# The predicated copies of a sorting network on VectorE walk their longest dimension innermost

## The chip, the cores and the metric

The kernel runs on one core of a Trainium2 chip. The metric is the device time of one execution in microseconds (us), the median of several runs; of the kernel before three runs are known.

## The reference, cut to what matters

The program is a two-layer relational graph convolution over 625 nodes of 768 features, followed by a feed-forward part with sixteen experts. The graph part and the output layers are not touched here. What matters is the gate of each expert:

```
for i in range(16):
    gate_feature = hidden_states * pe[i] @ gate_w + gate_b
    gate_weight, gate_idx = top_k(gate_feature, 384)      # of 768, for each of 625 tokens
    gate_weight = softmax(gate_weight)
    gathered = take_along_axis(hidden_states, gate_idx)
    y = y + (silu(x @ eg_w[i]) * (x @ eu_w[i])) @ ed_w[i]  # x = gathered * gate_weight
```

So for each expert and each token the largest 384 of 768 gate features are wanted in order, and with each of them the hidden value of the same column.

## The kernel before, in words

**The sort.** The kernel does the top_k as a sorting network on VectorE. The 625 tokens lie as 125 partitions by 5 tokens (`NT = 5`), so that each partition sorts 5 times 768 values at once. The 768 values of a token are three runs of 256 (`BLK = 3`), interleaved: the word at place i of run b of token t lies at `(i*3 + b)*5 + t` in a partition. One place of the three runs and five tokens is 15 words (`GRP = 15`). A stage of the network compares places that are `dist` apart; the function `pair` gives its two sides as views. For a stage of the first part (kind "sort", distances from 128 down to 1) a side has rows of `dist * 15` words at a pitch of twice that, except where `dist` is the length of the run that is merged. After the stage "join" the two best runs of each token lie in `key_top` and `pay_top` without the third run, and a place is 5 words: there the rows are `dist * 5` words at a pitch of twice that. In "join" and "flip" the outputs are contiguous, seen as rows of 5 words.

**Keys and payloads.** Keys (`key`, `key_top`) are the gate features, payloads (`pay`, `pay_top`) the hidden values. A unit of work is a stage or half of one, up to 960 words in a partition, in `UNITS`. For each unit VectorE does four instructions: the larger keys (a maximum, L1616), the smaller keys (a minimum, L1626), and two predicated copies that move the payloads under a mask, the first by `first_pays` (L1637, L1643 or L1649, after the kind of stage), the second by `second_pays` (L1657 or L1666). TensorE makes the mask in PSUM (L1218) from a seed that ScalarE puts there (L1507) and the larger keys, with a product by minus the identity: where the seed was the larger one the mask is zero. ScalarE (L1520) copies a part of the old payloads aside, and GpSimd computes the other part of the second payloads with a sum and a difference of integers (L1319, L1327), so the second copy on VectorE covers only part of the unit (`shares`).

**The order of the work.** The order is written out. There are an opening turn (74 units), fifteen regular turns (93 units each, thirteen of them in a loop) and a closing turn (19 units). A regular turn weaves the first part of one expert's sort with the last part of the sort of the expert before it, so that two chains alternate on VectorE: larger keys of unit u, second copy of unit u-2, smaller keys of u, first copy of unit u-1. TensorE does the experts' matrix products in between the masks. Each engine waits on semaphores of the others (`mask_made`, `seeded`, `moved`, `pays_done` and so on).

**The views.** `part_of` halves a stage, `in_banks` and `seed_of` give the mask the same dimensions as the payloads. A view of a copy has one to three free dimensions, for example `[2, 96, 5]` for the last merge stage: two halves, 96 rows, 5 words. A copy moves its elements in the order of these dimensions, the last one innermost, and that is the order that the change turns.

Of the kernel before, what the change touches and what calls it, by code (L numbers as in the profile page):

```python
# [208 lines left out]
def columns(view):  # L209

    return math.prod(view.shape[1:])


def shaped_like(buffer, view):

    dims = list(view.shape[1:])
    flat = buffer[:, 0:columns(view)]
    if len(dims) == 1:
        return flat
    if len(dims) == 2:  # L220
        return flat.rearrange("p (a b) -> p a b", b=dims[1])
    return flat.rearrange("p (a b c) -> p a b c", b=dims[1], c=dims[2])


def bank_pieces(view):
# [146 lines left out]
def settle(engine, waits_over):  # L372

    engine.sem_inc(waits_over, 1)
# [445 lines left out]
def experts(nc, ffn, chunks, ident, neg_ident, ones, pe_t, h_tok, h_feat, y_tok, gate_w, gate_b, gate_loaded,  # L820
            m1_loaded):
    with ExitStack() as ctx:
# [3 lines left out]
        def sem(name):  # L826
            return ctx.enter_context(nc.semaphore(name))
# [86 lines left out]
        pay_copied, moved, pays_done, pay_set = sem("pay_copied"), sem("moved"), sem("pays_done"), sem("pay_set")  # L914
# [56 lines left out]
        def pay_was(turn, u):  # L971

            home = (u % 2) * (NT * KTOP // 2)
            return shaped_like(pay_side[:, home:NT * KTOP], payloads(turn, u)[0])
# [4 lines left out]
        def seed_of(turn, u):  # L979


            side, bank = compared(turn, u)[0], mask_bank(turn, u)
            dims = list(side.shape[1:])
            if columns(side) <= BANK or len(dims) == 1:
                return shaped_like(bank, side)
            if dims[0] % 2 == 0:
                rows = bank.rearrange("p (n q) -> p n q", n=dims[0])[:, :, 0:math.prod(dims[1:])]
                return rows if len(dims) == 2 else rows.rearrange("p n (m x) -> p n m x", x=dims[2])
            if len(dims) == 3 and dims[0] == 1 and dims[2] // GRP * 16 <= BANK:
                rows = bank.rearrange("p (n m q) -> p n m q", n=1, q=dims[2] // GRP * 16)  # L990
                return rows[:, :, 0:dims[1], 0:dims[2]]
            return shaped_like(bank, side)
# [16 lines left out]
        def mask_of(turn, u):  # L1009
            return seed_of(turn, u).bitcast(I32)  # L1010
# [593 lines left out]
        @block.vector  # L1604
        def _(dve):
            def larger_keys(turn, i, u):
                s, part, _ = turn.units[u]
                dve.wait_ge(seeded, turn.done("units", i, u + 1))
                if s > 0:
                    dve.wait_ge(mask_made, turn.done("units", i, turn.needs[u]))  # L1610
                elif turn is not OPENING:
                    dve.wait_ge(maxed, turn.done("units", i, 0))
                    dve.wait_ge(minned, turn.done("minima", i, 0))
                if s == FLIP or (s == 0 and turn is not OPENING):
                    dve.wait_ge(kept, (i - 1) * NKEPT + 1)
                dve.tensor_tensor(results(turn, u)[0], seed_of(turn, u), compared(turn, u)[1],  # L1616
                                  ALU.max).then_inc(maxed, 1)

            def smaller_keys(turn, i, u):
                smaller, seed, second = results(turn, u)[1], seed_of(turn, u), compared(turn, u)[1]  # L1620
                if smaller is None:
                    return
                if turn.units[u][0] == JOIN:
                    seed, second = [side[:, 0:smaller.shape[1], :] for side in (seed, second)]
                dve.wait_ge(maxed, turn.done("units", i, u + 1))
                dve.tensor_tensor(smaller, seed, second, ALU.min).then_inc(minned, 1)  # L1626

            def first_pays(turn, i, u):

                s, part, parts = turn.units[u]  # L1630
                first, second, larger, _ = payloads(turn, u)
                dve.wait_ge(mask_made, turn.done("units", i, u + 1))
                if s == 0:
                    dve.wait_ge(pay_set, i * NSET + (part + 2))
                    settle(dve, sort_waits)
                    row_b = part_of(pair(h_mixed, None, STAGES[0])[1], part, parts)
                    dve.copy_predicated(first, mask_of(turn, u), row_b)  # L1637
                elif s == FLIP:
                    dve.wait_ge(pays_done, turn.done("units", i, turn.needs[u]))
                    dve.wait_ge(pays_taken, turn.done("sums", i, turn.needs[u]))  # L1640
                    dve.wait_ge(kept, i * NKEPT)
                    settle(dve, sort_waits)
                    dve.copy_predicated(larger, mask_of(turn, u), second).then_inc(pays_done, 1)  # L1643
                else:
                    dve.wait_ge(pay_copied, turn.done("moves", i, u + 1))
                    if turn.shared[u]:
                        dve.wait_ge(pays_added, turn.done("sums", i, u + 1))
                    settle(dve, sort_waits)
                    dve.copy_predicated(larger, mask_of(turn, u), second).then_inc(moved, 1)  # L1649

            def second_pays(turn, i, u):
                s, part, parts = turn.units[u]
                first, second, _, smaller = payloads(turn, u)
                mask = mask_of(turn, u)
                if s == 0:
                    row_a = part_of(pair(h_mixed, None, STAGES[0])[0], part, parts)
                    dve.copy_predicated(second, mask, row_a).then_inc(pays_done, 1)  # L1657
                elif s != FLIP:
                    was = pay_was(turn, u)
                    if s == JOIN:  # L1660
                        mask, was = mask[:, 0:smaller.shape[1], :], first[:, 0:smaller.shape[1], :]
                    elif turn.shared[u]:
                        smaller, mask, was = [shares(side, turn, u)[0] for side in (smaller, mask, was)]
                    dve.wait_ge(moved, turn.done("moves", i, u + 1))
                    settle(dve, sort_waits)
                    dve.copy_predicated(smaller, mask, was).then_inc(pays_done, 1)  # L1666

            def top_key(turn, i, u):
                dve.wait_ge(maxed, turn.done("units", i, u))
                dve.tensor_scalar(neg_max[:, :], key_top[:, 0:NT], -1.0, None, ALU.mult).then_inc(max_ready, 1)  # L1670

            def invert(e):
                dve.wait_ge(exp_ready, e * NT + NT)
                dve.reciprocal(exp_sum[:, :], exp_sum[:, :]).then_inc(inv_ready, 1)

            def sort(turn, i, following=None):

                for u in range(1, turn.streams):
                    if turn is REGULAR and u == INVERT:
                        invert(i - 1)  # L1680
                    larger_keys(turn, i, u)
                    if u > 1:
                        second_pays(turn, i, u - 2)
                    smaller_keys(turn, i, u)
                    if turn is REGULAR and u == SORTED + 1:
                        top_key(turn, i, SORTED + 1)
                    first_pays(turn, i, u - 1)
                if turn.streams:
                    second_pays(turn, i, turn.streams - 2)
                for u in range(max(turn.streams, 1), turn.n):  # L1690
                    larger_keys(turn, i, u)
                    smaller_keys(turn, i, u)
                    first_pays(turn, i, u - 1)
                    second_pays(turn, i, u - 1)
                if following is not None:
                    larger_keys(following, i + 1, 0)
                    smaller_keys(following, i + 1, 0)
                first_pays(turn, i, turn.n - 1)
                second_pays(turn, i, turn.n - 1)

            larger_keys(OPENING, 0, 0)
            smaller_keys(OPENING, 0, 0)
            sort(OPENING, 0, REGULAR)
            sort(REGULAR, 1, REGULAR)
            with dve.Fori(2, NEXP - 1) as i:
                sort(REGULAR, i, REGULAR)
            sort(REGULAR, NEXP - 1, CLOSING)
            sort(CLOSING, NEXP)
            top_key(CLOSING, NEXP, CLOSING.n)
            invert(NEXP - 1)  # L1710
# [120 lines left out]
```

## Time and profile before

| what | value |
|---|---|
| median of 3 runs | 6728.27 us |
| lowest and highest run | 6721.94 and 6728.85 us |
| span of the profiled execution | 6726.6 us |
| VectorE busy over the span | 5167.5 us (77%), 6633 instructions |
| TensorE busy over the span | 5752.0 us (86%) |
| GpSimd busy over the span | 4158.4 us (62%) |
| ScalarE busy over the span | 2659.1 us (40%) |

Of the profiled execution the page gives the span only, and no time of its own beside it; the span is 1.7 us under the median of the runs and lies between the lowest and the highest of them. "Busy" leaves out waiting, and a busy TensorE is not one at its peak. The share of busy time over the span hides that the kernel has different parts: the graph layers up to about 1215 us, then the sort. The rows further down are of the part in which the sort runs.

### The profile page before, as it was taken

To read this page: it belongs to the slowest core of one execution; us is meant where nothing else is said; L and a number is where in the kernel's file an instruction comes from. 1 tells how busy PE (TensorE), PEld (TensorE's weight loads), DVE (VectorE), ACT (ScalarE), POOL (GpSimd) and SP (SyncE) were. 2 spreads that over 40 slices of the span, in tenths; PEclk is the share of its full clock that TensorE was granted. 3 is DMA by queue.
4 is the path that set the end of the run, shared out by engine and by line. 5 is a ranking of instruction groups with operands and counts; after the bars stand their busy time and mean duration, and the time that the engine had idled before them with its cause. 6 is when DMAs were issued, how large, how long until landed. Compare 5 with 4: busy or idle time off the path is not lost. (4 is left out here: it accounts for less than half of the span.)

```text
span 6726.6 us, 73995 instructions
## 1 busy us (share of the span) xinstructions
PE 5752.0 (86%) x16753; PEld 3063.2 (46%) x16753; DVE 5167.5 (77%) x6633; ACT 2659.1 (40%) x4419; POOL 4158.4 (62%) x3692
## 2 busy tenths in 40 slices
PE   7979989788888888888888888888888888889988
PEld 5545545344444444444444444444444444445554
DVE  3012002399999999999999999999999999998840
ACT  0000000244545554454545454545454545554431
POOL 2325005266877777676777777777777777777740
PEclk9989999899999999999999999999999999999989
DMA  3357238100000000000000000000000000001001
GB/s 90 107 132 188 101 99 196 56 15 8 20 23 15 15 15 15 15 15 15 15 15 14 15 14 15 15 19 10 29 0 29 14 15 15 15 29 36 18 32 51
DMA packets 118084, 261.01 MB, mean 39 GB/s; under 512 B 39164, under 2 KB 49922, under 8 KB 117682
## 3 DMA queue, kind: packets, MB, share of 16 engines
q1 hardware_dynamic: 70322, 180.18, 7.6%
q0 software_dynamic: 47360, 77.17, 5.2%
q14 instruction: 357, 2.92, 0.1%
q8 instruction: 45, 0.74, 0.0%
HBM read 222.43 MB, written 34.58 MB: 38 GB/s over the span
## 5 line engine op out<-in xcount | busy, mean ns | idle before, releaser
L1218 PE MATMUL mask_ps<-key,neg_ident 125*125 125x480 f32 (+7 forms) x4128 | 1886.1, 575 | 567.4 <-DVE key L1626 561.2
L1327 POOL TENSOR_TENSOR pay<-pay_side,pay 125x480 int32<-125x480 int32 (+9 forms) x1120 | 1306.1, 1166 | 648.1 <-DVE pay L1649 641.0
L1507 ACT COPY mask_ps<-key 125x960 f32<-125x960 f32 (+7 forms) x1152 | 954.7, 829 | 1698.7 <-DVE pay L1666 1029.3
L1319 POOL TENSOR_TENSOR pay_side<-pay 125x480 int32<-125x480 int32 (+9 forms) x1120 | 1301.1, 1162 | 340.6 <-DVE pay L1666 160.9
L1218 PEld LDWEIGHTS mask_ps<-key,neg_ident 125*125 125x125 f32 x4128 | 732.8, 192 | 1459.8 <-DVE key L1626 994.5
L1649 DVE COPY_PREDICATED pay<-mask_ps,pay 125x960 f32<-125x960 int32 (+6 forms) x1120 | 1240.7, 1108 | 69.0 <-PE mask_ps L1218 35.5
L1616 DVE TENSOR_TENSOR key<-mask_ps,key 125x960 f32<-125x960 f32 (+6 forms) x1120 | 1092.4, 975 | 57.5 <-PE mask_ps L1218 36.2
L1626 DVE TENSOR_TENSOR key<-mask_ps,key 125x960 f32<-125x960 f32 (+6 forms) x1120 | 1092.8, 976 | 0.0
L1218 PE MATMUL mask_ps<-key_top,neg_ident 125*125 125x480 f32 (+3 forms) x1472 | 604.1, 539 | 178.2 <-DVE key_top L1626 168.0
L1165 PE MATMUL slot_ps<-w_exp,hid 128*125 128x384 f32 x1920 | 680.4, 493 | 8.7 <-issue 8.7
L1153 PE MATMUL slot_ps<-gate_w,xs 128*125 128x384 f32 x1920 | 678.8, 490 | 0.0
L1137 PE MATMUL slot_ps<-u_feat,w_exp 128*128 128x312 f32 (+1 forms) x2304 | 668.2, 427 | 0.4 <-ACT u_feat L1397 0.4
L758 POOL DMA_INDIRECT rows_a<-messages_dram,idx_now_a x200 | 242.3, 1212 | 660.6 <-DVE idx_now_a L795 612.7
L657 PE MATMUL ps_msg<-w_rel,h_feat 128*125 128x384 f32 x1920 | 619.7, 486 | 2.4 <-ACT h_feat L589 2.4
L1666 DVE COPY_PREDICATED pay<-mask_ps,pay_side 125x480 f32<-125x480 int32 (+8 forms) x1120 | 592.1, 529 | 4.8 <-DVE pay L1649 2.9
L1520 ACT COPY pay_side<-pay 125x480 f32<-125x480 f32 (+8 forms) x1120 | 508.6, 454 | 147.0 <-POOL pay L1327 97.6
L1137 PEld LDWEIGHTS slot_ps<-u_feat,w_exp 128*128 128x128 f32 x2304 | 439.7, 191 | 245.0 <-issue 119.0
L668 DVE COPY y_out<-ps_msg 125x768 f32<-125x768 f32 x40 | 38.3, 958 | 612.2 <-PE ps_msg L657 612.2
L1165 PEld LDWEIGHTS slot_ps<-w_exp,hid 128*125 128x125 f32 x1920 | 366.4, 191 | 306.9 <-issue 114.7
L1327 POOL TENSOR_TENSOR pay_top<-pay_side,pay_top 125x480 int32<-125x480 int32 (+3 forms) x272 | 327.5, 1204 | 281.1 <-DVE pay_top L1649 276.8
L1153 PEld LDWEIGHTS slot_ps<-gate_w,xs 128*125 128x125 f32 x1920 | 359.1, 189 | 306.1 <-issue 120.8
L1218 PEld LDWEIGHTS mask_ps<-key_top,neg_ident 125*125 125x125 f32 x1472 | 270.8, 199 | 489.1 <-DVE key_top L1626 289.7
(190 smaller groups left out, 5876.3 us busy)
## 6 DMA issues: line engine op xcount, KB each, us to landing
w_rel<-L_gnn_W SPq DMA_DIRECT2D x16, 2304.0 KB, 23.2
w_exp<-L_ffn_ed_w SPq DMA_DIRECT2D x16, 2304.0 KB, 8.4
messages_dram<-y_out SPq DMA_DIRECT2D x16, 1875.0 KB
w_exp<-L_ffn_eg_w SPq DMA_DIRECT2D x16, 1152.0 KB, 5.4
w_exp<-L_ffn_eu_w SPq DMA_DIRECT2D x16, 1152.0 KB, 7.8
root_w<-L_gnn_root SPq DMA_DIRECT2D x2, 2304.0 KB
w_exp<-L_ffn_sg_w SPq DMA_DIRECT2D x4, 1152.0 KB, 6.0
w_exp<-L_ffn_su_w SPq DMA_DIRECT2D x4, 1152.0 KB, 8.8
```

The lines of the kernel that those rows point to most:

```text
L657: last = pe.matmul(slots[n % 2][0:TP, half, 0:HALF], h_feat[:, k, t * TP:(t + 1) * TP], w_rel[j][:, k, cols], start=(k == 0), stop=(k == K ...
L1137: last = pe.matmul(slots[bank][:, 0:count], weight(bank, k), ins[:, k, first:first + count], start=(k == 0), stop=(k == nk - 1))
L1153: last = pe.matmul(slot, xs[:, t % 2, k, :], gate_w[:, k, cols], start=False, stop=(k == KD - 1), skip_group_check=is_set(e, t))
L1165: last = pe.matmul(slots[bank][0:TP, 0:HALF], hid[:, f, t * TP:(t + 1) * TP], down_w[:, f, half * HALF:(half + 1) * HALF], start=(f == 0), ...
L1218: last = pe.matmul(mask, neg_ident[0:TP, 0:TP], operand, start=False, stop=True, skip_group_check=True)
L1319: pool.tensor_tensor(shares(pay_was(turn, u), turn, u)[1].bitcast(I32), first, second, ALU.add).then_inc(pays_added, 1)
L1327: pool.tensor_tensor(second, shares(pay_was(turn, u), turn, u)[1].bitcast(I32), first, ALU.subtract).then_inc(pays_taken, 1)
L1507: act.copy(seed_of(turn, u), compared(turn, u)[0]).then_inc(seeded, 1)
L1616: dve.tensor_tensor(results(turn, u)[0], seed_of(turn, u), compared(turn, u)[1], ALU.max).then_inc(maxed, 1)
L1626: dve.tensor_tensor(smaller, seed, second, ALU.min).then_inc(minned, 1)
L1649: dve.copy_predicated(larger, mask_of(turn, u), second).then_inc(moved, 1)
L1666: dve.copy_predicated(smaller, mask, was).then_inc(pays_done, 1)
```

## The change

A new function turns the views of a predicated copy. It looks for the longest of the output's free dimensions (the first of them, where two are equal) and, where that isn't the innermost already, puts it innermost in output, mask and data alike. All five predicated copies go through it. The same elements are copied under the same mask; only their order within an instruction differs. Copies whose last dimension is the longest, or that have one dimension alone, stay as they are.

```diff
+def longest_last(*views):
+
+    dims = list(views[0].shape[1:])
+    longest = dims.index(max(dims))
+    if longest == len(dims) - 1:
+        return views
+    names = ["abc"[n] for n in range(len(dims))]
+    turned = names[:longest] + names[longest + 1:] + [names[longest]]
+    order = f"p {' '.join(names)} -> p {' '.join(turned)}"
+    return [view.rearrange(order) for view in views]
...
-                    dve.copy_predicated(first, mask_of(turn, u), row_b)
+                    dve.copy_predicated(*longest_last(first, mask_of(turn, u), row_b))
...
-                    dve.copy_predicated(larger, mask_of(turn, u), second).then_inc(pays_done, 1)
+                    dve.copy_predicated(*longest_last(larger, mask_of(turn, u), second)).then_inc(pays_done, 1)
...
-                    dve.copy_predicated(larger, mask_of(turn, u), second).then_inc(moved, 1)
+                    dve.copy_predicated(*longest_last(larger, mask_of(turn, u), second)).then_inc(moved, 1)
...
-                    dve.copy_predicated(second, mask, row_a).then_inc(pays_done, 1)
+                    dve.copy_predicated(*longest_last(second, mask, row_a)).then_inc(pays_done, 1)
...
-                    dve.copy_predicated(smaller, mask, was).then_inc(pays_done, 1)
+                    dve.copy_predicated(*longest_last(smaller, mask, was)).then_inc(pays_done, 1)
```

An example: the first copy of the last merge stage has the view `[2, 96, 5]`, 192 rows of 5 words at a pitch of 10. Turned it is `[2, 5, 96]`: ten walks of 96 elements, each element 10 words behind the last.

## Rows read from the trace of the kernel before

**Rows 1.** The page's engines: busy us, share of the span, instructions.
```profile
PE 5752.0 (86%) x16753; PEld 3063.2 (46%) x16753; DVE 5167.5 (77%) x6633; ACT 2659.1 (40%) x4419; POOL 4158.4 (62%) x3692
```

**Rows 2.** Busy time by stretch, from the first join to the last; columns in its first line.
```profile
core 0: us, PE busy (x) PEld busy (x) DVE busy (x) ACT busy (x) POOL busy (x), PEclk, DMA share, GB/s
1549.00:6395.00 4846.00, 4113.28 (x11583) 2119.73 (x11583) 4612.19 (x5553) 2395.86 (x4004) 3568.18 (x3130) 0.96 0.05 17
```

**Rows 3.** Waits of VectorE: waiter, whom for, us in total, times, longest.
```profile
DVE key L1616 <- ACT mask_ps L1507: 99.1, 28, 79.1
DVE key_top L1616 <- PE mask_ps L1218: 56.8, 41, 3.1
DVE pay L1649 <- PE mask_ps L1218: 35.5, 25, 10.6
DVE pay_top L1649 <- ACT pay_top L1518: 24.2, 16, 1.6
DVE pay L1637 <- PE mask_ps L1218: 14.0, 18, 1.5
```

**Rows 4.** VectorE, 2527 to 2849 us, in order of time: start us, us, instruction.
```profile
2533.70 1.43 DVE L1637 COPY_PREDICATED pay<-mask_ps,h_tok 125x960 f32<-125x960 int32 x1 [0.75 <-PE mask_ps L1218]
...
2542.06 1.32 DVE L1649 COPY_PREDICATED pay<-mask_ps,pay 125x960 f32<-125x960 int32 x1
...
2552.15 1.25 DVE L1649 COPY_PREDICATED pay_top<-mask_ps,pay_top 125x960 f32<-125x960 int32 x1
...
2555.99 0.88 DVE L1649 COPY_PREDICATED pay<-mask_ps,pay 125x480 f32<-125x480 int32 x1
...
2557.27 0.34 DVE L1666 COPY_PREDICATED pay<-mask_ps,pay_side 125x120 f32<-125x120 int32 x1
...
2565.40 1.25 DVE L1649 COPY_PREDICATED pay_top<-mask_ps,pay_top 125x960 f32<-125x960 int32 x1
...
2567.62 0.66 DVE L1666 COPY_PREDICATED pay_top<-mask_ps,pay_side 125x480 f32<-125x480 int32 x1
...
2569.26 1.21 DVE L1649 COPY_PREDICATED pay<-mask_ps,pay 125x960 f32<-125x960 int32 x1
...
2571.44 0.67 DVE L1666 COPY_PREDICATED pay<-mask_ps,pay_side 125x480 f32<-125x480 int32 x1
...
2573.09 1.42 DVE L1649 COPY_PREDICATED pay_top<-mask_ps,pay_top 125x960 f32<-125x960 int32 x1
2574.38 1.14 DVE L1616 TENSOR_TENSOR key_top<-mask_ps,key_top 125x960 f32<-125x960 f32 x1
...
2576.10 1.15 DVE L1626 TENSOR_TENSOR key_top<-mask_ps,key_top 125x960 f32<-125x960 f32 x1
...
2579.72 1.92 DVE L1649 COPY_PREDICATED pay_top<-mask_ps,pay_top 125x960 f32<-125x960 int32 x1
...
2582.23 1.00 DVE L1666 COPY_PREDICATED pay_top<-mask_ps,pay_side 125x480 f32<-125x480 int32 x1
...
2834.98 0.88 DVE L1649 COPY_PREDICATED pay_top<-mask_ps,pay 125x640 f32<-125x640 int32 x1 [1.57 <-ACT pay_top L1518]
```

**Rows 5.** Line 357 on VectorE: count, shortest/median/longest ns, first and last start.
```profile
L357 DVE TENSOR_SCALAR h_tok<-x_tok,mean_var,rstd x5: 674/676/679, 100.9 to 103.2; 125x768 f32<-125x768 f32 x5
L357 DVE TENSOR_SCALAR h_tok<-x_tok,mean_var_a,rstd_a x5: 1543/1547/1569, 1212.0 to 1217.6; 125x768 f32<-125x768 f32 x5
```

**Rows 6.** Groups of instructions: count, busy us, mean ns, then idle time before.
```profile
L1649 DVE COPY_PREDICATED pay<-mask_ps,pay 125x960 f32<-125x960 int32 x320 | 403.2, 1260 | 31.9 <-POOL pay_side L1319 24.3 <-PE mask_ps L1218 5.7 <-ACT pay_side L1520 1.6
L1616 DVE TENSOR_TENSOR key<-mask_ps,key 125x960 f32<-125x960 f32 x320 | 366.7, 1146 | 36.2 <-PE mask_ps L1218 36.2
```

## The prediction, made before the changed kernel had run

> **What bounds the kernel now.** I read the engines' busy shares first. TensorE has the larger share over the whole span, 86% against VectorE's 77% [rows 1], and that misleads, because the span has parts in which VectorE has next to nothing to do. The busy time by stretch puts it right: between the first join at 1549 us and the last at 6395 us, fifteen regular turns, VectorE is busy 4612 of 4846 us, 95%, TensorE 4113 (85%), GpSimd 3568 (74%), ScalarE 2396 (49%) [rows 2]. A turn is 4846 / 15 = 323 us. The waits of VectorE in this part are small and scattered, the largest kinds being tens of us in all [rows 3]; of the first, 99.1 us, 79.1 are one wait at the start. So in 72% of the span whatever is added to VectorE's stream or taken from it comes out in the time nearly whole. The question is what one of them costs in either order.
>
> **What a predicated copy costs now.** A copy of 960 elements takes 1.26 us in the mean of its largest group, the maximum of the same shape 1.15 [rows 6]. The mean hides a spread, and the order of time shows it. With the code I can say what each row of [rows 4] walks in its output, and that sorts them:
>
> - rows of 80, of 60 or of 20 words, 960 elements: 1.25, 1.21, 1.25 us (starts 2552.15, 2569.26, 2565.40); 480 elements in rows of 60 or 20: 0.67, 0.66 (2571.44, 2567.62)
> - rows of 30, 960 elements: 1.32 (2542.06)
> - rows of 15, 960 elements: 1.43 (2533.70); 480 elements in 32 rows, each starting three words past a multiple of four: 0.88 (2555.99); 120 elements in 8 rows: 0.34 (2557.27)
> - rows of 10, 960 elements: 1.42 (2573.09)
> - rows of 5, 960 elements: 1.92 (2579.72); 480 elements: 1.00 (2582.23)
> - a join, 640 elements, output contiguous, data in rows of 5 at a pitch of 15: 0.88 (2834.98)
>
> Rows of 20 cost nothing extra and rows of 30 do, so the length of a row alone isn't it; nor is it the data's rows (the join). What fits all is the number of aligned groups of four words (16 bytes, "lines" below) that the output touches. 960 words in rows of 80, 60 or 20 touch 240 lines; rows of 30 touch 8 lines each, 256; rows of 15 at a pitch of 30 touch 4 and 5 in turn, 288; rows of 10 touch 3 each, 288; rows of 5 at a pitch of 10 touch 2 each, 384. The short ones: 480 words in full lines 120, the 480 in rows of 15 from word 3 on 5 each, 160, the rows of 5 192, the join 160, the 120 words 40. A straight line through the thirteen copies gives 0.134 us + 4.58 ns per line and misses none by more than 0.04 us; I use 4.55 ns. The number of elements adds nothing: 480 elements (160 lines) and 640 elements (160 lines) both take 0.88 us. The unpredicated instructions don't do this: the maximum and the minimum on the same rows of 5 take 1.14 and 1.15 us [rows 4], what any 960 take [rows 6]. So it is a price of the predicated write, paid once per line whether one or four of its words are written.
>
> **The change part by part.** It adds and removes no instruction, wait or DMA. From the code, 49 of the 184 predicated copies of a regular turn have their longest dimension elsewhere than last: 25 in rows of 15, 6 in rows of 30, 4 each in rows of 20, 10 and 5, and the 6 of join and flip, whose contiguous output is seen as rows of 5. With opening and closing turn that makes 785 copies, with 554,305 elements in all, that touch 163,820 lines. After the change the step from one element to the next is 30 or 60 words in the first part of the sort (120 in one stage), 40, 20 or 10 in the merges, and 5 in join and flip: always over four, so each element goes to another line than the one before it, and 554,305 elements are 554,305 visits to a line.
>
> - Removed: nothing that the output lines don't count already. In [rows 4] the end of a row as such is free (rows of 20, rows of 80).
> - Added: 554,305 - 163,820 = 390,485 visits. No predicated copy of the kernel before steps like this, so its price has to be bounded. Lower end: the price that an element has in full lines now, 4.55 / 4 = 1.14 ns, if the line does not matter in a stepped walk. Next: the one VectorE instruction that writes with a step, line 357 of the second graph layer, 768 elements at a step of 15 words in 1547 ns [rows 5]; less the fixed 0.13 us that is 1.84 ns an element (the same line written contiguously takes 676 ns). Upper end: 4.55 ns a line and on top the 0.8 ns that the step costs over 1.04 ns an element in line 357, 5.35 ns.
> - I take 4.55 ns. It is the only price of the right kind of instruction, and the partial lines in the rows bear it out: a row of 5 is one full line and one of a single word, or two lines of two and three words, and a row of 10 has one of two words, and all are priced like full ones.
> - Sum: 390,485 x 4.55 ns = 1777 us. A stretched copy of 960 elements is then 0.13 + 4.37 = 4.5 us in place of 1.2 to 1.9.
> - What lies beside it: a longer copy gives TensorE and ScalarE time for the next mask and seed. The waits for masks and for ScalarE's copies in the join (56.8 + 35.5 + 24.2 + 14.0 = 130 us) [rows 3] can shrink; about half of them stand within three instructions of a turned copy, so I take off 65 us.
> - Other engines: GpSimd and ScalarE wait for the copies' semaphores. GpSimd had 26% of the stretch free, ScalarE half; both chains alternate on VectorE, so a longer copy of one delays the other as well and nobody but VectorE becomes late. TensorE gets idler.
>
> Total: 6727 + 1777 - 65 = 8439 us against the profiled span, 8440 beside the median. About 0.2%, 13 us, is what a measurement here can tell from nothing.
>
> **Two rules weighed.** Steps cost something in unpredicated writes too: line 357 shows 1.84 ns an element [rows 5]. The Trainium skill says so ("Vector Engine (DVE) Microarchitecture Reference", Measured stream behaviour on trn2): a port keeps its full rate only on adjacent, aligned pairs of words; a write that hops every element took 1.71 ns, one at steps of 24 words 2.50. By this trace's row the rule holds for a plain write, and the rule knows nothing of a predicate. At its 2.5 ns the turned copies would cost 1386 us, an estimate from that page, 640 more than now. And the 16-byte group that fits the rows above is named there too ("SBUF — State Buffer", Door 1: The DMA port swizzle): consecutive accesses to the same 16-byte line are the fast ones. The trace agrees on the 16 bytes, for predicated writes alone.
>
> **Rivals.**
> 1. *The step costs what a plain stepped write costs.* The line's price would be one of leaving a row, and in a stepped walk the write would run at line 357's rate. For it: that is VectorE's only stepped write in the trace. Against it: partial lines in the middle of the sort cost full price, and plain writes on the same rows cost nothing extra. 554,305 x 1.84 ns = 1020 us against 163,820 x 4.55 = 745 now: +275, some 15 of it in waits, 6990 us. With the page's dearer steps up to 7350.
> 2. *The other side: short rows are the price and steps are free.* Rows of 5 cost 0.67 us more than rows of 80, rows of 15 0.2 more; if this is a restart at a row's end, 96 elements in a walk buy it back. Then the turned copies cost 554,305 x 1.14 = 632 us, 113 less, nearly all in the time: 6617 us. It decides from a price under 745 / 554.3 = 1.34 ns an element. For it: short rows are dear, and few long walks end seldom. Against it: rows of 20 are free and rows of 30 aren't, join and flip have nothing to win, being contiguous, and line 357 shows steps that aren't free.
> 3. *Line price and step price add up*, in output, mask and data: 5.35 ns or more; 554,305 x 5.35 = 2966, +2220: 8880 us after the same 65.
> 4. *The change doesn't do what it says*: the dimensions could be put back in order on the way to the instruction, and nothing would move: 6728 us. Nothing in the trace speaks for it.
>
> **How the numbers follow.** Forecast 55% (its own range 8300 to 8600), rival 1 20%, rival 2 12%, rival 3 10%, rival 4 3%. The range for 8 in 10 leaves out rivals 2 and 4 (15%) and the far end of rival 3: 6900 to 8950 us. It is wide because the two prices of a stepped write are far apart. Faster 0.12, the same 0.03, slower 0.85.
>
> **What would show it.** In the changed kernel's profile the group of line 1649 with 960 elements splits into copies of about 1.23 us that stay and copies near 4.5 us; the copies of 640 elements in join and flip go from the 0.88 of [rows 4] to 3.0 us; they are the purest case, contiguous before. Line 1616 stays at 1.15. VectorE's busy share in the sort goes to 97% or more and TensorE's falls to about 63%. A turn takes near 430 us. If these 640 show about 1.3 us it is rival 1; at 0.88 still, rival 2; if a 960 in rows of 15 shows 1.2 us where it showed 1.43, rows were the price. Wrong altogether would be a time that the copies' durations don't account for: then an engine that waits for them has become the bound.

## The result and the profile after

The changed kernel takes 8383.6 us, the median of 4 runs (8379.8 to 8393.2), against 6728.6 us for the kernel before beside it: a ratio of 1.2466 with a 95% interval of 1.245 to 1.2482, 1655 us more. The forecast was 8440 us.

The engines of the changed kernel, as in [rows 1]:

```profile
span 8391.4 us, 73995 instructions
PE 6292.5 (75%) x16753; PEld 3269.0 (39%) x16753; DVE 6839.1 (82%) x6633; ACT 2658.6 (32%) x4419; POOL 4160.8 (50%) x3692
```

The number of instructions is the one of before. VectorE has 1672 us more of work (6839.1 - 5167.5), GpSimd and ScalarE have what they had. TensorE has 540 us more busy time without one more instruction; more on that below.

The fifteen regular turns, in a stretch that answers to [rows 2] (columns: us, then busy time and count of PE, PEld, DVE, ACT, POOL, then the granted clock of TensorE, DMA share, GB/s). Under it the copy that opens each join, first of before, then of after: its last two times are the start of the first join's first copy and that of the last join's second one, 15 turns and 2 us apart in both kernels.

```profile
1615.00:8029.00 6414.00, 4631.06 (x11582) 2316.11 (x11583) 6176.99 (x5553) 2395.45 (x4005) 3568.88 (x3130) 0.86 0.04 13
```
```profile
L1518 ACT COPY pay_top<-pay x32: 486/650/797, 1549.7 to 6395.7; 125x640 f32<-125x640 f32 x16, 125x320 f32<-125x320 f32 x16
```
```profile
L1530 ACT COPY pay_top<-pay x32: 487/645/803, 1615.4 to 8029.6; 125x640 f32<-125x640 f32 x16, 125x320 f32<-125x320 f32 x16
```

A turn takes about (8029.6 - 1615.4) / 15 = 427.6 us, before (6395.7 - 1549.7) / 15 = 323.1 us; the 2 us drop out of the difference, 104.5 us. VectorE is busy 6177 of 6414 us, 96.3%.

The groups of copies and of maxima, by shape (count, busy us and mean ns, idle time before and what ended it). Lines are 12 further down than before: L1661 is L1649 of before, L1649 is L1637, L1655 is L1643, L1678 is L1666, L1628 is L1616.

```profile
L1661 DVE COPY_PREDICATED pay<-mask_ps,pay 125x930 f32<-125x930 int32 x80 | 337.8, 4222 | 0.6 <-ACT pay_side L1532 0.6
L1649 DVE COPY_PREDICATED pay<-mask_ps,h_tok 125x960 f32<-125x960 int32 x32 | 141.2, 4414 | 12.8 <-PE mask_ps L1230 12.7
L1661 DVE COPY_PREDICATED pay_top<-mask_ps,pay 125x640 f32<-125x640 int32 x32 | 97.3, 3042 | 13.1 <-ACT pay_top L1530 13.1
L1655 DVE COPY_PREDICATED pay_top<-mask_ps,u_feat 125x640 f32<-125x640 int32 x16 | 48.2, 3010 | 0.0
L1661 DVE COPY_PREDICATED pay<-mask_ps,pay 125x840 f32<-125x840 int32 x144 | 166.1, 1154 | 6.5 <-issue 2.6 <-PE mask_ps L1230 2.3 <-ACT pay_side L1532 0.9
L1628 DVE TENSOR_TENSOR key<-mask_ps,key 125x840 f32<-125x840 f32 x144 | 146.3, 1016 | 4.1 <-ACT mask_ps L1519 4.1
```

Copies of 930 and 960 elements whose walk was turned take 4.2 to 4.4 us. The join's copies of 640, 0.88 us before [rows 4], take 3.04, and line 1655, the flip, the same. The 144 copies of 840 elements are not turned and are as short as ever, and the maxima too. A single one of each kind that stood in [rows 4], at its new time (start us, us):

```profile
3936.95 4.35 DVE L1661 COPY_PREDICATED pay_top<-mask_ps,pay_top 125x960 f32<-125x960 int32 x1
3940.94 1.34 DVE L1628 TENSOR_TENSOR key<-mask_ps,key 125x960 f32<-125x960 f32 x1
3942.21 2.24 DVE L1678 COPY_PREDICATED pay_top<-mask_ps,pay_side 125x480 f32<-125x480 int32 x1
```

The last merge stage, in rows of 5 words before, went from 1.92 to 4.35 us, its second copy from 1.00 to 2.24. The maximum behind such a copy shows 1.34 us for 1.15, but it also begins 0.36 us before the copy's end; counted from start to start, the two together take no more than the copy's own lengthening.

### The profile page after: what moved, and what is told of

Read it like the earlier page. It is cut to its first block and busy times, and to the rows that moved or that the text cites. A ratio compares the mean times of both kernels' runs of the same rounds, so it can differ in the third digit from the quotient of the medians.

```text
span 8391.4 us, 73995 instructions
## 1 busy us (share of the span) xinstructions
PE 6292.5 (75%) x16753; PEld 3269.0 (39%) x16753; DVE 6839.1 (82%) x6633; ACT 2658.6 (32%) x4419; POOL 4160.8 (50%) x3692
## 5 line engine op out<-in xcount | busy, mean ns | idle before, releaser
L1230 PE MATMUL mask_ps<-key,neg_ident 125*125 125x480 f32 (+7 forms) x4128 | 2124.6, 638 | 1287.4 <-DVE key L1638 1281.4
L1661 DVE COPY_PREDICATED pay<-mask_ps,pay 125x960 f32<-125x960 int32 (+6 forms) x1120 | 2006.1, 1791 | 136.9 <-PE mask_ps L1230 105.5
L1230 PEld LDWEIGHTS mask_ps<-key,neg_ident 125*125 125x125 f32 x4128 | 789.0, 209 | 2302.9 <-DVE key L1638 1801.5
L1628 DVE TENSOR_TENSOR key<-mask_ps,key 125x960 f32<-125x960 f32 (+6 forms) x1120 | 1153.0, 1029 | 31.2 <-PE mask_ps L1230 25.0
L1230 PE MATMUL mask_ps<-key_top,neg_ident 125*125 125x480 f32 (+3 forms) x1472 | 701.0, 611 | 575.1 <-DVE key_top L1638 509.5
L1638 DVE TENSOR_TENSOR key<-mask_ps,key 125x960 f32<-125x960 f32 (+6 forms) x1120 | 1122.2, 1002 | 0.0
L1165 PE MATMUL slot_ps<-gate_w,xs 128*125 128x384 f32 x1920 | 757.4, 536 | 0.0
L1177 PE MATMUL slot_ps<-w_exp,hid 128*125 128x384 f32 x1920 | 743.8, 529 | 8.6 <-issue 8.6
L1678 DVE COPY_PREDICATED pay<-mask_ps,pay_side 125x480 f32<-125x480 int32 (+8 forms) x1120 | 742.8, 663 | 4.8 <-DVE pay L1661 2.9
L1661 DVE COPY_PREDICATED pay_top<-mask_ps,pay_top 125x960 f32<-125x960 int32 (+1 forms) x272 | 616.4, 2266 | 17.7 <-PE mask_ps L1230 9.0
L1519 ACT COPY mask_ps<-key_top 125x960 f32<-125x960 f32 (+1 forms) x304 | 275.5, 906 | 885.7 <-DVE pay L1678 527.0
```

Source lines behind the costliest of these rows:

```text
L1165: last = pe.matmul(slot, xs[:, t % 2, k, :], gate_w[:, k, cols], start=False, stop=(k == KD - 1), skip_group_check=is_set(e, t))
L1177: last = pe.matmul(slots[bank][0:TP, 0:HALF], hid[:, f, t * TP:(t + 1) * TP], down_w[:, f, half * HALF:(half + 1) * HALF], start=(f == 0), ...
L1230: last = pe.matmul(mask, neg_ident[0:TP, 0:TP], operand, start=False, stop=True, skip_group_check=True)
L1519: act.copy(seed_of(turn, u), compared(turn, u)[0]).then_inc(seeded, 1)
L1661: dve.copy_predicated(*longest_last(larger, mask_of(turn, u), second)).then_inc(moved, 1)
L1678: dve.copy_predicated(*longest_last(smaller, mask, was)).then_inc(pays_done, 1)
```

## The experiments

All are made from the kernel before or the changed one. "Visits" are the times at which the walk of an output enters an aligned group of four words (16 bytes).

**The price of the copy by itself.** VectorE alone, behind the last stage of the kernel before, each instruction waiting for the last one.

```diff
+    probe(nc)   # behind output(...)
+            for _ in range(4):
+                link(copy(to[:, 0:640], mask[:, 0:640], data[:, 0:640]))          # L1844
...
+                link(copy(every(to, 2), mask[:, 0:640], data[:, 0:640]))          # L1848, 3: L1849, 4: L1850, 5: L1851, 6: L1852
...
+                link(copy(to[:, 0:640], mask[:, 0:640], every(data, 5)))          # L1855
+                link(copy(to[:, 0:640], every(mask, 3), data[:, 0:640]))          # L1856
+                link(copy(rows(to, 4, 8), like(mask, 4), like(data, 4)))          # L1857
+                link(copy(rows(to, 4, 8, 2), like(mask, 4), like(data, 4)))       # L1858, two words later
...
+                link(dve.tensor_tensor(every(to, 5), mask[:, 0:640].bitcast(F32), data[:, 0:640], ALU.max))   # L1862
```

> The kernel before, and after its last stage a block in which VectorE alone does 21 instructions of 640 elements (two of 320) four times over, each waiting for the one before; time of the whole doesn't matter. Theory L (each visit of the output to an aligned group of four words costs 4.4 to 4.55 ns on top of 0.13 us, nothing else counts): contiguous 0.86 us (320 elements 0.50), the same with a mask of zeros and with the mask in SBUF; output at a step of 2 words (two elements per line, 320 visits) 1.57 us, at a step of 3 (480 visits) 2.3, at steps of 4, 5 and 6 (640 visits) 3.0 us each, also with a mask of zeros; data alone at a step of 5, or mask alone at a step of 3, 0.86 us; rows of 4 words on line starts 0.86, the same rows two words later (two lines each, 320 visits) 1.57; rows of 2 words at a pitch of 4 1.57, one word later still 1.57. Rival S (a stepped walk is slow per element, whatever the lines, and rows pay for their ends): steps of 2 to 6 all near 3.0 us, data at a step of 5 as slow as the output, rows of 4 the same at either start. Rival R (the price is the reads of mask and data, not the write): data or mask alone at a step take 2 us or more, output alone at a step takes under 1.5. The four maxima: contiguous 0.8 us, output at a step of 5 about 1.3 us (1.84 ns an element as in line 357), data at a step of 5 about the same.

The groups of that block, mean ns in the fourth number (L1853 is a step of 5 with a mask of zeros, L1854 320 elements at a step of 5, L1845 320 contiguous, L1861 a contiguous maximum):

```profile
L1851 DVE COPY_PREDICATED to_p<-mask_p,data_p 125x640 f32<-125x640 int32 x4 | 12.0, 2993 | 0.1
L1853 DVE COPY_PREDICATED to_p<-zero_p,data_p 125x640 f32<-125x640 int32 x4 | 12.0, 2992 | 0.1
L1850 DVE COPY_PREDICATED to_p<-mask_p,data_p 125x640 f32<-125x640 int32 x4 | 12.0, 2989 | 0.1
L1852 DVE COPY_PREDICATED to_p<-mask_p,data_p 125x640 f32<-125x640 int32 x4 | 11.8, 2959 | 0.1
L1849 DVE COPY_PREDICATED to_p<-mask_p,data_p 125x640 f32<-125x640 int32 x4 | 9.1, 2286 | 0.1
L1848 DVE COPY_PREDICATED to_p<-mask_p,data_p 125x640 f32<-125x640 int32 x4 | 6.3, 1575 | 0.1
L1858 DVE COPY_PREDICATED to_p<-mask_p,data_p 125x640 f32<-125x640 int32 x4 | 6.3, 1574 | 0.1
L1854 DVE COPY_PREDICATED to_p<-mask_p,data_p 125x320 f32<-125x320 int32 x4 | 6.3, 1569 | 0.1
L1862 DVE TENSOR_TENSOR to_p<-mask_p,data_p 125x640 f32<-125x640 f32 x4 | 5.2, 1292 | 0.1
L1855 DVE COPY_PREDICATED to_p<-mask_p,data_p 125x640 f32<-125x640 int32 x4 | 5.1, 1284 | 0.1
L1856 DVE COPY_PREDICATED to_p<-mask_p,data_p 125x640 f32<-125x640 int32 x4 | 3.5, 868 | 0.1
L1844 DVE COPY_PREDICATED to_p<-mask_p,data_p 125x640 f32<-125x640 int32 x4 | 3.5, 867 | 0.1
L1857 DVE COPY_PREDICATED to_p<-mask_p,data_p 125x640 f32<-125x640 int32 x4 | 3.3, 831 | 0.1
L1861 DVE TENSOR_TENSOR to_p<-mask_p,data_p 125x640 f32<-125x640 f32 x4 | 3.3, 825 | 0.1
L1845 DVE COPY_PREDICATED to_p<-mask_p,data_p 125x320 f32<-125x320 int32 x4 | 2.1, 514 | 0.1
```

It is the visits. 640 elements at a step of 2, in 4-word rows across a line's edge, and 320 elements at a step of 5 all make 320 visits and all take 1.57 us. The same 4-word rows on the line's start make 160 and take 0.83. Steps of 4, 5 and 6 cost alike, 2.96 to 2.99, a step of 3 (480 visits) 2.29. A visit costs (2993 - 1569) / 320 = 4.45 ns. A mask of zeros saves nothing, a stepped mask costs nothing. That the price is the step's whatever the lines (rival S), or that of reading mask and data (rival R), is refuted. One forecast missed: data alone at a step of 5 take 1.28 us and not 0.86, the time of the stepped maximum. So a stepped read has a price of its own, but a smaller one.

**One part of the change at a time.** Join and flip, then the merges, then the rest, each by the condition in `longest_last`:

```diff
-    if longest == len(dims) - 1:
+    if longest == len(dims) - 1 or dims[-2:] != [64, 5]:                            # join and flip
+    if longest == len(dims) - 1 or dims[-2:] not in ([96, 5], [48, 10], [24, 20]):  # merges
+    if longest == len(dims) - 1 or dims[-2:] in ([64, 5], [96, 5], [48, 10], [24, 20]):   # the rest
```

> The change for the copies of join and flip alone, 96 copies whose output is contiguous before and stepped by 5 words after: visits to lines rise from 14,080 to 56,320, by 42,240. Theory L: +42,240 x 4.4 ns = +186 us, near 6915 us; each copy of 640 elements 0.88 to 3.0 us. Rival S' (only what is already short-rowed gets dear; contiguous copies with a small step stay in the reach of few lines and cost the plain stepped price of 1.84 ns): +56,320 x 1.84 - 64 = +40 us, 6768 us. Rival W (waits decide, the copies of the join sit beside waits for ScalarE that absorb them): under +120 us though the copies take 3 us.

Measured 6894.8 us beside 6724.1, ratio 1.0257 (1.0236 to 1.0277), +171 us. The 32 copies of the join take 3030 ns in the median. Their output covers 160 lines in either order; it is the 640 visits that cost. The forecast of 186 us was 15 too high, though the copies cost what was forecast: VectorE's busy time rose by 184 us (5167.5 to 5351.6), and its waits shrank a little. Rival S' with 40 us is out, and so is rival W.

> The change for the 192 copies of the merge stages with rows of 5, 10 and 20 words alone: visits rise from 43,776 to 138,240, by 94,464. Theory L: +94,464 x 4.37 ns = +413 us, near 7140 us, all of them near 4.4 us whether their rows were free (20) or dear (5) before. Rival R2 (end of a row is a price of its own, so rows of 5 gain part of it back): rows of 5 turned clearly cheaper than rows of 20 turned, by 0.5 us or more, and the sum under +350 us.

Measured 7160.0 us, ratio 1.0651 (1.063 to 1.0673), +436 us. In the order of time the turned first copies whose rows were 20, 10 and 5 words take 4.22, 4.38 and 4.37 us; before they took 1.25, 1.42 and 1.92 [rows 4]. What their rows were no longer shows, so rival R2 is out. The copies account for 401 us: the rows below against 305.1 us for the first copies and 145.2 for the second ones in the same groups of before. The waits make up the rest, for masks before all: 28.9 us ahead of these copies, 8.2 in the kernel before.

```profile
L1661 DVE COPY_PREDICATED pay_top<-mask_ps,pay_top 125x960 f32<-125x960 int32 x224 | 573.1, 2559 | 42.3 <-PE mask_ps L1230 28.9 <-issue 6.0 <-ACT pay_side L1532 2.9
L1678 DVE COPY_PREDICATED pay_top<-mask_ps,pay_side 125x480 f32<-125x480 int32 x192 | 278.7, 1452 | 1.8 <-DVE pay_top L1661 1.7
```

> The change for the copies with rows of 15 and 30 words alone (497 copies of the sort's first part, two and three dimensions); join, flip and merges stay. Visits rise by 253,781. The block after the kernel before gave 4.43 ns for each further visit of a stepped output and 4.41 for a full line, the merges alone +436 us for 94,464 visits (4.6 ns, waits for masks among them), join and flip alone +171 for 42,240 (4.05 ns). Theory L with parts that add: 8384 - 6728 - 171 - 436 = 1049 us here, near 7775 us, 4.13 ns a visit. Theory L without interplay (the copies' price alone): +253,781 x 4.35 = +1104 us, near 7830. Rival (the parts hide in one another, so that this part alone costs nearly what the whole does): above 7950.

Measured 7804.1 us beside 6723.9, ratio 1.1604 (1.1583 to 1.1625), +1080 us, between the two forecasts of theory L. The three parts add up to 171 + 436 + 1080 = 1687 us for the 1655 of the whole: they add, within 2%.

**The outer order alone.** The two outer dimensions exchanged, the innermost left in place.

```diff
-    if longest == len(dims) - 1:
+    if longest == len(dims) - 1 or len(dims) < 3:
         return views
...
-    turned = names[:longest] + names[longest + 1:] + [names[longest]]
+    turned = [names[1], names[0], names[2]]
```

> The copies that the change turns and that have three free dimensions get their two outer dimensions exchanged, while the innermost stays; two-dimensional ones stay as before. Nothing is stepped. Visits change for join and flip alone: their contiguous output becomes rows of 5 out of order, 256 lines for 160 in a copy of 640, +7680 visits in all. Theory L: join and flip copies of 640 elements take 0.13 + 256 x 4.5 ns = 1.29 us instead of 0.88, all other copies as before, the whole +34 us (+0.5%), 6762 us. Rival S (only a step between neighbouring elements costs): no copy moves, within 0.1% of before. Rival O (order of far jumps costs by itself): merges with rows of 5, which now jump 960 words between rows, get slower than 1.92 us too, and the whole by more than 60 us.

Measured 6760.9 us, ratio 1.0052 (1.0035 to 1.0069), +37 us (24 to 46 by the interval) for 34 forecast. No neighbouring elements are stepped here, and yet join and flip get slower, by the 96 visits more that rows of 5 make when they don't follow one another (shortest/median/longest ns):

```profile
L1661 DVE COPY_PREDICATED pay_top<-mask_ps,pay x32: 1300/1314/1333, 1559.0 to 6442.0; 125x640 f32<-125x640 int32 x32
```

1314 ns where 0.13 + 256 x 4.5 ns makes 1.29 us. This is the line's price without any step. The merges' copies, whose rows now lie far apart in order but make the same visits, stay as they were: their group of 224 takes 304.8 us for 305.1, so far jumps cost nothing by themselves (rival O).

**Can the price be put to use?** In the merges with rows of 10 and 5 GpSimd takes more of the second payloads, so that VectorE makes fewer visits.

```diff
     eighths = 3 if u >= turn.streams else 6 if turn is REGULAR and u in turn.free else 4
+    if STAGES[turn.units[u][0]][0] in ("merge", "bitonic_tail") and STAGES[turn.units[u][0]][2] in (1, 2) and turn is REGULAR:
+        dim, eighths = 2, 6
```

> The kernel before, with the price per line put to use: in the merge stages with rows of 10 and 5 words GpSimd computes six eighths of the second payloads in place of four, cut along the rows, and VectorE's second copy shrinks from 480 to 240 elements. Theory L: each of the four copies of a turn loses 72 or 96 visits, 336 a turn, 1.5 us, 15 turns: -23 us, 6701 us. Rival P (GpSimd is late then: a sum and a difference of 720 elements take 1.65 us each for 1.2 now, 3.6 us more a turn, in front of copies that wait for it): no gain or slower by up to 40 us, with waits for GpSimd's payloads in VectorE's list.

Measured 6720.8 us beside 6723.9, ratio 0.9996 (0.9987 to 1.0005): no difference. The copies did get shorter as forecast, from 145.2 us to 91.9 + 31.7:

```profile
L1668 DVE COPY_PREDICATED pay_top<-mask_ps,pay_side 125x480 f32<-125x480 int32 x132 | 91.9, 696 | 1.8 <-DVE pay_top L1651 1.8
L1668 DVE COPY_PREDICATED pay_top<-mask_ps,pay_side 125x240 f32<-125x240 int32 x60 | 31.7, 529 | 0.0
```

The 22 us came back as waits of VectorE (us in all, times, longest). The same three were 35.5 [rows 3], 24.3 [rows 6] and 5.8 us in the kernel before, 24 us less together:

```profile
DVE pay L1651 <- PE mask_ps L1220: 43.6, 45, 10.4
DVE pay L1651 <- POOL pay_side L1321: 34.8, 51, 0.8
DVE pay L1651 <- ACT pay_side L1522: 11.5, 16, 1.7
```

VectorE had 23 us less of work in the whole run (5167.5 to 5144.4), GpSimd 58 us more (4158.4 to 4216.3), and the time didn't move. That is rival P's outcome, no gain. But its cause, that GpSimd comes late, is seen for only 10.5 of the 24 us; 8.1 are for masks and 5.7 for ScalarE's copies. Whether a copy made shorter without more work for GpSimd would pay wasn't tried. No version faster than the kernel before came out of the study.

**Where the price lies.** The same kind of block with other outputs.

```diff
+                link(copy(every(to, 5), every(mask, 3), every(data, 5)))                        # L1851
+                link(copy(every(to, 10, 384), mask[:, 0:384], every(data, 10, 384)))            # L1852
+                link(copy(half_to[:, 0:640], mask[:, 0:640], half_data[:, 0:640]))              # L1854, two bytes
+                link(copy(every(half_to, 2), mask[:, 0:640], half_data[:, 0:640]))              # L1855
+                link(copy(ps_to[:, 0:640], mask[:, 0:640], data[:, 0:640]))                     # L1856, output in PSUM
+                link(copy(every(ps_to, 2, 512), mask[:, 0:512], data[:, 0:512]))                # L1857
+                link(dve.tensor_tensor(every(to, 2), mask[:, 0:640].bitcast(F32), data[:, 0:640], ALU.max))   # L1858, 3: L1859, 4: L1860
```

> The kernel before, and after its last stage VectorE alone, 13 instructions four times over. Theory L and the larger of two prices: output and data both at a step of 5 words, 640 elements, mask contiguous or at a step of 3, 2.99 us as with the output alone (read and write beside one another), not 2.99 + 0.42; 384 elements at a step of 10 words 1.85 us; 128 at a step of 30 0.70 us; both by 0.13 + 4.45 ns an element. Two-byte output and data, 640 contiguous (80 lines): if lines alone count 0.49 us, if an element costs its 1.04 ns at least 0.80; at a step of 2 elements (160 lines) 0.84. Output in PSUM: 0.86 us contiguous if the price is the predicate's, about 0.7 to 0.8 if it is the SBUF write's. The maxima, whose output at a step of 5 took 1.29 us: at a step of 2 0.83 (pairs of words share 16 bytes), at 3, 4 and 6 up to 1.3; output and data both at a step of 5: 1.3 if they overlap, 1.75 if they add.

```profile
L1851 DVE COPY_PREDICATED to_p<-mask_p,data_p 125x640 f32<-125x640 int32 x4 | 12.1, 3018 | 0.1
L1860 DVE TENSOR_TENSOR to_p<-mask_p,data_p 125x640 f32<-125x640 f32 x4 | 5.1, 1282 | 0.1
L1859 DVE TENSOR_TENSOR to_p<-mask_p,data_p 125x640 f32<-125x640 f32 x4 | 4.0, 1000 | 0.1
L1855 DVE COPY_PREDICATED half_to_p<-mask_p,half_data_p 125x640 bf16<-125x640 int32 x4 | 3.5, 870 | 0.1
L1856 DVE COPY_PREDICATED ps_to_p<-mask_p,data_p 125x640 f32<-125x640 int32 x4 | 3.3, 832 | 0.1
L1854 DVE COPY_PREDICATED half_to_p<-mask_p,half_data_p 125x640 bf16<-125x640 int32 x4 | 3.3, 827 | 0.1
L1858 DVE TENSOR_TENSOR to_p<-mask_p,data_p 125x640 f32<-125x640 f32 x4 | 3.3, 824 | 0.1
L1857 DVE COPY_PREDICATED ps_to_p<-mask_p,data_p 125x512 f32<-125x512 int32 x4 | 2.8, 699 | 0.1
```

Stepped data beside a stepped output add nothing (3.02 us for 2.99), so the larger price counts. At a step of 10, 384 such elements take 1.84 us, again 4.4 ns each on top of the fixed part. With two-byte elements the lines are few and the elements themselves set the time (0.83 us; 0.87 at 160 visits). An output in PSUM doesn't show the line price: 512 elements at a step of 2 enter 256 aligned groups, which would be 0.13 + 256 x 4.45 ns = 1.27 us in SBUF, and take 0.70 us, 133 ns less than 640 contiguous for 128 elements less. The contiguous copy alone, 0.83 us beside 0.87 in SBUF and 0.7 to 0.8 forecast, wouldn't have decided it, and wider steps in PSUM weren't run. So the price is that of the predicated write to SBUF.

## Why the prediction was right, point by point

**The bound.** Right. VectorE was the bound and stayed it; 1655 us of the time stand against 1672 us more of its work, and no other engine turned up in its place.

**The price of a visit.** The mechanism was right. The size was 5% off: forecast 4.55 ns for each of 390,485 further visits, measured, over the 49 turned copies of one turn of the loop, 105.7 us longer for 24,354 visits, 4.34 ns. A stage-0 copy went from 1.43 [rows 4] to 4.41 us for 672 visits, 4.45 ns each; one of the merge with rows of 5 from 1.92 to 4.35 us for 576, 4.2 ns each. The forecast took the slope among copies whose lines were mostly full and laid it on lines of one word. Alone on the engine both cost the same (4.41 ns between 320 and 640 contiguous elements, (867 - 514) / 80, and 4.45 ns stepped), so the 4.55 of before holds something that isn't the line's; what, the runs don't settle. In the fifteen turns the difference is 77 us too much in the forecast.

**What lies beside it.** This step failed, by 65 us the other way. VectorE's idle time in the fifteen turns was 234 us before (4846 - 4612) and 237 after (6414 - 6177). The four kinds of waits of which half was to go made 130 us and make 138. The larger keys' wait for masks fell from 56.8 to 6.3 us (19.1 us stand at the same instruction now for which the profile names no engine), the join's from 24.2 to 13.1, that of line 1649 (1637 before) from 14.0 to 12.7. Those for masks ahead of the first copies grew from 35.5 to 105.5 us:

```profile
DVE pay L1661 <- PE mask_ps L1230: 105.5, 85, 8.1
DVE key_top L1628 <- PE mask_ps L1230: 6.3, 10, 2.2
DVE pay_top L1661 <- ACT pay_top L1530: 13.1, 16, 0.9
```

Why masks come later although TensorE has more time shows in the order of time behind the stretched copies at 3936.95 and 3942.21 us, first of the changed kernel, then of the kernel before at the same place of the turn (start us, us, the last bracket is idle time before):

```profile
3945.49 2.88 PE L1230 MATMUL mask_ps<-key,neg_ident 125*125 125x480 f32 x4 [4.05 <-DVE key L1638]
3949.07 3.56 PE L1230 MATMUL mask_ps<-key,neg_ident 125*125 125x480 f32 x4 [0.70 <-DVE key L1638]
```
```profile
3294.86 1.88 PE L1218 MATMUL mask_ps<-key,neg_ident 125*125 125x480 f32 x4 [1.84 <-DVE key L1626]
3298.44 1.88 PE L1218 MATMUL mask_ps<-key,neg_ident 125*125 125x480 f32 x4 [1.71 <-DVE key L1626]
```

and the stretches with their granted clock, the third number from the right:

```profile
3945.50:3949.00 3.50, 2.87 (x4) 0.80 (x4) 3.50 (x5) 3.41 (x6) 2.82 (x3) 0.60 0.00 0
3949.00:3953.00 4.00, 3.93 (x5) 1.82 (x6) 2.62 (x6) 3.24 (x7) 3.86 (x4) 0.50 0.00 0
```
```profile
3298.40:3302.00 3.60, 3.56 (x10) 1.98 (x11) 3.60 (x5) 2.95 (x6) 3.60 (x3) 1.00 0.00 0
```

TensorE stood idle 4.05 us while VectorE copied, 1.84 before; then its granted clock was 0.60 and 0.50, mostly and then wholly the lower of its two levels, 1.2 GHz for 2.4. The same four products took 3.56 us for 1.88, and the copy at 3952.97 waited 1.38 us for that mask.

The largest part of the growth lies elsewhere: one copy of a turn waits 2.91 us in each of the thirteen turns of the loop, 37.8 of the 70 us, and never waited for its mask before. First the changed kernel, then the kernel before at the same place:

```profile
3276.04 2.45 PE L1230 MATMUL mask_ps<-key,neg_ident 125*125 125x480 f32 x4 [2.00 <-DVE key L1638]
3279.99 4.19 PE L1165 MATMUL slot_ps<-gate_w,xs 128*125 128x384 f32 x6
3286.02 1.16 DVE L1661 COPY_PREDICATED pay<-mask_ps,pay 125x900 f32<-125x900 int32 x1 [2.91 <-PE mask_ps L1230]
```
```profile
2807.93 1.88 PE L1218 MATMUL mask_ps<-key,neg_ident 125*125 125x480 f32 x4 [2.00 <-DVE key L1626]
2810.57 2.20 PE L1153 MATMUL slot_ps<-gate_w,xs 128*125 128x384 f32 x6
```

Here too the clock made the mask late: it was 0.53 from 3277 to 3280 us and 0.50 from 3280 to 3283, against 1.00 before (2809 to 2812), and the six products of the gate that run ahead of the mask's took 4.19 us for 2.20. But TensorE's idle time ahead of it, 2.00 us, is the same in both kernels, so a longer gap just before doesn't explain this fall.

Over the turns the granted clock is 0.86 for 0.96 [rows 2], and that ratio accounts for nearly all of the 518 us by which TensorE is busier there (4113 x 0.96 / 0.86 = 4591 of 4631 us). That slower products made the masks late is read from these places of the trace. That the longer copies, by the idle time that they leave TensorE, brought the clock down is likely from the first place, and isn't shown by the second. To keep TensorE busy in the gaps with products of no effect would have tested it, and was not tried.

**The sum.** Forecast for the visits 1777 us, 1662 of them in the fifteen turns (15 x 24,354 x 4.55 ns) and 115 outside; the spans differ by 8391.4 - 6726.6 = 1665. The turns brought 6414.2 - 4846.0 = 1568 us, 94 under the forecast: 77 for the smaller price (15 x (110.8 - 105.7)), and 17 that the copies' durations don't show. These lie at both ends: from join to join the first turn is 99.2 us longer and the last 93.4, the thirteen between 104.7 to 106.9, which is what the copies add. Outside the turns it was 97 for 115, and 6 of these 18 us are no effect of the change: line 357 of the second graph layer, line 369 now, began at 1205.7 us for 1212.0 [rows 5] before any copy was turned. That the waits gave nothing back, 65 us, made up for most of it, so the total of 8440 us is nearer (0.7%) than its two terms, and that is luck.

**The rivals.** Rival 1 is refuted by the blocks: a plain stepped write costs 1.28 us where the predicated one costs 2.99. The Trainium skill's rule on plain writes ("Vector Engine (DVE) Microarchitecture Reference", Measured stream behaviour on trn2) agrees in part. Its 1.71 ns for a write that hops at every element stands beside 1.77 ns here ((1282 - 150) / 640, with 0.15 us for the fixed part). But by it the full rate needs runs of at least two adjacent words, and here a maximum at a step of 2 words, where no two are adjacent, takes 0.82 us, as long as a contiguous one (825 ns): in this the measurement decides against the page. Rival 2 fell by the free rows of 20 already and finally by the 4-word rows at either start, 0.83 and 1.57 us. Rival 3 is refuted: a stepped output costs the line price and no more, and read and write prices overlap. Its 5.35 ns rested on a misreading, too: it set 1.04 ns an element as the unstepped price of line 357, where the same line written contiguously, 676 ns for 768 elements [rows 5], gives 0.71; the step added 1.13 ns there, and the bound would have been 5.7. The 4.55 ns don't hang on it. Rival 4 is out by the result.

**The shares.** Forecast 97% for VectorE and 63% for TensorE in the turns, measured 96.3% and 72%: the difference at TensorE is nearly all its clock. A turn took 427.6 us for 430.

## What to carry to other kernels

A predicated copy into SBUF is priced by how often its output enters an aligned 16-byte group, about 4.4 ns each. For two-byte elements, with few lines, it is the element that counts, at about 1.04 ns (maxima of 480 and 960 elements take 646 and 1146 ns in the kernel before); count these visits from the views before changing an order, and keep four-byte outputs in runs that start and end on multiples of four words. Mean durations over one shape hide this: sort the instructions of one turn by the strides that the code gives them. And don't count on a slower bound engine to win back its own waits: here VectorE's idle time stayed at 234 and 237 us, as TensorE's products ran at a lower granted clock.

## What the runs showed of the hardware that was not expected

- An output in PSUM doesn't show such a price: 0.83 us for 640 elements, 0.70 for 512 at a step of 2.
- Plain writes to SBUF go by the same lines with a lower price: a maximum over 640 elements takes 0.82 us at a step of 2 words (320 visits), 1.00 at 3 (480), 1.28 at 4 (640). 1.77 ns a visit fits the last two, and at 320 visits the elements' 1.04 ns are the larger.
- A line that is entered again is paid again: a join's 160 lines, entered 640 times, take 3.03 us, as 640 different lines do in the block (2.99).
- Four-word rows on line starts with gaps between them are a little quicker than one contiguous run over as many lines, 831 ns for 867.
